# A scan layer on Trainium2: B is expanded straight from PSUM, in one go, and B and C are projected ahead of delta

## The reference, cut to what matters

```python
proj  = seq @ W_proj.T + b_proj                   # seq: (16, 1024, 192)
x_in, delta, Bm, Cm = split(proj, [192, 192, 16, 16])
delta = softplus(delta + dt_bias)
A     = -exp(A_log)                               # (192, 16)
# for every step t:
h     = exp(delta[t, :, None] * A) * h + (delta[t] * x_in[t])[:, None] * Bm[t, None, :]
y[t]  = sum over states of h * Cm[t]
out   = (y + x_in * D) @ W_out.T + b_out
```

## Time and profile before

| | us |
|---|---|
| median of 3 runs | 4584.7 (4575.44 to 4586.21) |
| profiled execution, its own time | 4598.03 |
| its span, first to last instruction | 4596.2 |
| busy: PE, DVE, ACT, POOL | 4019.0, 3294.0, 2112.8, 2494.7 |
| mean granted clock of TensorE | 0.921 |
| scans of both scan layers | from 1791.5 on, about 60% of the span |

### The profile page before, as it was taken

The page is one execution under the profiler, slowest core; times in us unless marked ns, Lnnn a source line. Parts: engine busy times, 40 slices in busy tenths (PEclk is TensorE's granted clock), DMA queues, the critical chain, the costliest instruction groups (busy, mean ns, idle before and its releaser), DMA issues. The chain is left out here.

```text
span 4596.2 us, 165194 instructions
## 1 busy us (share of the span) xinstructions
PE 4019.0 (87%) x71984; PEld 2447.8 (53%) x71984; DVE 3294.0 (72%) x3495; ACT 2112.8 (46%) x2773; POOL 2494.7 (54%) x877
## 2 busy tenths in 40 slices
PE   5994899999999966999999989995899899999998
PEld 4993666666666643444444444442454444444444
DVE  6655666767576634887877877873788778888786
ACT  2331444443434434555555555552555455555553
POOL 1111212121111203887877878883788778888886
PEclk9997999999999986899999999996799999999998
DMA  9623324233232413444434434432444444444342
GB/s 100 88 41 94 107 64 119 73 107 85 83 108 73 112 28 87 99 97 98 108 88 97 109 88 100 112 75 64 99 94 107 94 95 102 97 100 111 83 96 65
DMA packets 371280, 419.28 MB, mean 91 GB/s; under 512 B 31818, under 2 KB 284494, under 8 KB 370562
## 3 DMA queue, kind: packets, MB, share of 16 engines
q1 hardware_dynamic: 370596, 408.83, 39.2%
HBM read 267.23 MB, written 91.16 MB: 78 GB/s over the span
## 5 line engine op out<-in xcount | busy, mean ns | idle before, releaser
L1143 POOL TENSOR_TENSOR l_h<-l_h,l_c_rep 128x2048 f32<-128x2048 f32 x384 | 1768.8, 4606 | 210.3 <-DVE l_h L1062 208.3
L767 PEld LDWEIGHTS l_u_ps<-l_b_diag,l_dx_t 32*64 32x64 f32 x49152 | 836.9, 139 | 704.1 <-issue 701.3
L1062 DVE TENSOR_TENSOR_SCAN l_h<-l_decay,l_u_ps 128x512 f32<-128x512 f32 x768 | 891.3, 1201 | 376.9 <-PE l_y_ps L780 341.1
L767 PE MATMUL l_u_ps<-l_b_diag,l_dx_t 32*64 32x64 f32 x49152 | 948.5, 227 | 187.0 <-issue 105.3
L902 ACT ACTIVATE l_decay<-l_delta_rep,l_a_neg 128x1024 f32<-128x1024 f32 x768 | 858.1, 1143 | 405.3 <-DVE l_h L1062 400.4
L1062 DVE TENSOR_TENSOR_SCAN l_h<-l_decay,l_h,l_u_ps 128x512 f32<-128x512 f32 x768 | 932.0, 1254 | 9.7 <-PE l_u_ps L767 9.6
L780 PE MATMUL l_y_ps<-l_h,l_state_sum 128*64 128x512 f32 x3072 | 858.4, 685 | 11.1 <-POOL l_h L1143 11.1
L1673 ACT ACTIVATE l_probs<-l_work 128x532 f32<-128x532 f32 (+1 forms) x384 | 217.6, 567 | 559.7 <-PE l_work L1527 553.0
L780 PEld LDWEIGHTS l_y_ps<-l_h,l_state_sum 128*64 128x64 f32 x3072 | 205.0, 149 | 307.5 <-issue 264.1
L1086 DVE TENSOR_TENSOR l_b_diag<-l_b_t,l_lane 128x1024 f32<-128x1024 f32 x128 | 314.6, 2461 | 54.8 <-ACT l_b_t L954 54.8
L1842 DVE RECIPROCAL l_den<-l_den 96x1024 f32<-96x1024 f32 x32 | 209.6, 6549 | 196.3 <-ACT l_den L1686 196.3
(11 more groups left out here) (162 smaller groups left out, 5785.1 us busy)
## 6 DMA issues: line engine op xcount, KB each, us to landing
l_c_rep<-l_c_by_state SPq DMA_DIRECT2D x256, 512.0 KB, 6.5
l_delta_rep<-l_delta SPq DMA_DIRECT2D x384, 128.0 KB, 5.4
l_x<-x_after_l SPq DMA_DIRECT2D x48, 768.0 KB, 5.7
l_qk_parts<-l_qk SPq DMA_DIRECT2D x48, 768.0 KB, 4.8
l_x_res<-x_after_l SPq DMA_DIRECT2D x192, 128.0 KB
l_x<-x SPq DMA_DIRECT2D x64, 192.0 KB, 9.5
x_after_l<-l_x SPq DMA_DIRECT2D x64, 192.0 KB, 4.1
l_x_res<-x_after_l SPq DMA_DIRECT2D x16, 768.0 KB, 5.4
```

The lines of the kernel that those rows point to most:

```text
L767: made = nc.tensor.matmul(u_ps[64 * par:64 * par + 64, w % U_RING, r - 2 * win, at:at + 64], dx_t[rows, n.s, db, k, 64 * g:64 * g + 64], b ...
L1062: nc.vector.tensor_tensor_scan(h[:, s % S_RING, npi, t], decay[:, 2 * (s % 2) + npi, t], u, start, ALU.mult, ALU.add).then_inc(scanned, 1)
L1143: nc.gpsimd.tensor_tensor(view, view, c_rep[:, 2 * q:2 * q + 2, :], ALU.mult).then_inc(c_applied, 1)
```

## The change

`take_b`, ACT's copy of the transposed B out of the scratch bank into `b_t`, is gone, and with it `b_t` and the semaphore `diag_made`. DVE's `diagonals` waits for the fill itself and reads the bank. All four quarters are made one after the other behind window 11, and the last one counts the bank as drained; `fill_u` waits for that count. In the table, `bc` and `bt` move from slots 13 and 14 to 9 and 10, `de.0` from 11 to 13, and `tail.2`, the third output tile, from 9 to 14. POOL's list follows: the third residual addition goes from step 4 to 6, `finish_delta` from steps 6, 8, 9 to 7, 9, 10, `make_dx` from 7, 10 to 8, 11.

```diff
     slots = {
-        1: ["x.2"], 2: ["dx.1"], 3: ["norm"], 5: ["tail.0"], 6: ["dx.2"], 7: ["tail.1"], 9: ["tail.2"], 11: ["de.0"],
-        13: ["bc"], 14: ["bt"], 15: ["x.0"], 17: ["de.1"], 19: ["de.2"], 20: ["dx.0"], 21: ["x.1"],
+        1: ["x.2"], 2: ["dx.1"], 3: ["norm"], 5: ["tail.0"], 6: ["dx.2"], 7: ["tail.1"], 9: ["bc"], 10: ["bt"],
+        13: ["de.0"], 14: ["tail.2"], 15: ["x.0"], 17: ["de.1"], 19: ["de.2"], 20: ["dx.0"], 21: ["x.1"],
     }
...
                     if w == 0:
-                        pe.wait_ge(diag_made, n.count(1, 1))
+                        await_drained(pe, fill(n, "bt"))
...
-                def take_b(n):
-                    f = fill(n, "bt")
-                    await_fill(act, f)
-                    nc.scalar.activation(b_t[:, :], scratch[:, 0:256], ACT.Copy).then_inc(drained, 1)
-
...
                     if npq == 0:
-                        await_drained(dve, fill(n, "bt"))
-                    b = b_t[:, :].rearrange("p (c m) -> p c m", c=16)[:, :, 2 * npq:2 * npq + 2]
+                        await_fill(dve, fill(n, "bt"))
+                    b = scratch[:, 0:256].rearrange("p (c m) -> p c m", c=16)[:, :, 2 * npq:2 * npq + 2]
...
                     if npq == 3:
-                        made.then_inc(diag_made, 1)
+                        made.then_inc(drained, 1)
...
-                        if w in (16, 17, 18, 20):
-                            diagonals(after(n), (16, 17, 18, 20).index(w))
+                        if w == 11:
+                            for npq in range(4):
+                                diagonals(after(n), npq)
...
-                    if s in (2, 3, 4) and not n.first:
-                        add_residual(before(n), s - 2)
+                    if s in (2, 3, 6) and not n.first:
+                        add_residual(before(n), (2, 3, 6).index(s))
                     if not last:
-                        if s in (6, 8, 9):
-                            finish_delta(after(n), (6, 8, 9).index(s))
-                        if s in (7, 10):
-                            make_dx(after(n), s // 10)
+                        if s in (7, 9, 10):
+                            finish_delta(after(n), (7, 9, 10).index(s))
+                        if s in (8, 11):
+                            make_dx(after(n), s // 11)
```

More of the change, by code:

```diff
@@ L502, in ssm_layer @@
         b_rows = sb("b_rows", [64, HALF])
-        b_t = sb("b_t", [128, 256])
         c_rows = sb("c_rows", [128, HALF])
@@ L561, in ssm_layer @@
         dx_made = sem("dx_made")
-        diag_made = sem("diag_made")
         rows_seen = sem("rows_seen")
@@ L988, in take_slot @@
                             take_bc(of)
-                        elif kind == "bt":
-                            take_b(of)
                         elif kind == "x":
@@ L994, in take_slot @@
                             take_dx(of, int(i))
-                        else:
+                        elif kind == "tail":
                             take_output(before(n), int(i))
@@ L1004, in prologue @@
                     take_bc(n)
-                    take_b(n)
                     take_x(n, 0)
```

## The result

| | before | after |
|---|---|---|
| median, us | 4585.45 (4 runs, 4575.44 to 4588.27) | 4881.45 (4 runs, 4865.79 to 4892.88) |
| ratio | 1 | 1.0657, 95% interval 1.0626 to 1.0688 |
| profiled execution, span | 4596.2 | 4876.0 |
| mean granted clock | 0.921 | 0.882 |
| busy: PE, DVE, ACT, POOL | 4019.0, 3294.0, 2112.8, 2494.7 | 4182.4, 3148.6, 2089.7, 2396.6 |

The kernel became 6.6% slower, 296 us. The forecast of 4647 us had the sign, but the time lies far above its range, which ended at 4740. DVE and POOL lost 145 and 98 us of work, as wanted; the same matmuls kept TensorE busy for 163 us more, at a mean granted clock of 0.882 instead of 0.921.

The account below looks back on a forecast made before the run. TensorE bounds the scan layers, through its holes and clock. Per batch +3.1 - 2.6 + 2.85 - 1.5 = +1.8 us, +54 in 30 batches, +8 for prologues: 4584.7 + 62 = 4647 us, range 4555 to 4740.

Parts of the forecast that it names:

- The block's price: DVE's four diagonals in a row, read from the scratch bank: 1.11 us each, 4.44 us for the block.
- the estimate of 0.26 us more of fixed cost for the four: DVE's diagonals: by the skill's errata table, a PSUM source costs 62 cycles more, about 0.26 us for the four.
- The prologues' 8 us: Once a layer, x.0's fill waits for the diagonals: +4.2 us each less ACT's copy, +8 us in all.
- TensorE's holes for DVE at the batch's end: TensorE's waits for DVE's scans there would go: at most 2.6 us a batch, and 1.5 us of clock behind them.
- The place and the size of the stall: TensorE waits 3.1 us once a batch at window 15's u fill, for the scans of window 12 behind the block.
- SP's chain to delta 0: From POOL's last addition through SP's store, loads and C store to the end of delta 0's issues: 16.6 us.
- Hidden, with 1.2 us to spare: Batch start: first scans end 27.1 us after the third output tile; TensorE needs them after 28.3 us, so no cost.
- which nothing in my sum moves: TensorE's "issue" waits would stay at 3.6 us a batch.
- The third rival: SP's chain overruns its 1.2 us at batch starts, C loads without pause: +3 us a batch, 4737 us, chance 0.17.
- my case: Main forecast for the whole kernel: 4647 us, own range 4600 to 4707, chance 0.48.
- the clock behind the stall: Low clock behind the block's stall costs 2.85 us a batch, from eight stretches behind the loop's branch (1.65 to 4.8).
- The gain: At the batch's end, 2.6 us of waits for DVE and 1.5 us of clock go, per batch.

Follow-up runs that it names:

- the square: e5, e9, e10 and the changed kernel: third output tile in window 9 or 14, without or with the stall; ratios to before 0.990, 1.011, 1.043, 1.066.
- e5: Changed kernel with the third output tile back in slot 9 and the block of diagonals two windows later, behind window 13: 4531.84 us, ratio to before 0.990.
- e8: Changed kernel with the third output tile in slot 9, the block behind window 15, and bc, de.0, bt, x.0 in 11, 12, 13, 16: 4535.46 us.
- e2: Changed kernel with a sixteenth of the bytes in the loop batches' loads of C (the rest of C stale): 4622.94 us.
- e6: Kernel before the change with the loop batches' loads of C cut to 64 of 1024 columns (C stale): 4495.47 us.
- e9: e5 with the third output tile back in slot 14 and delta's first projection moved to 16: 4628.68 us, ratio to before 1.011.
- e10: Changed kernel with the third output tile in slot 9, B and C moved to 8, the block still behind window 11: 4770.76 us, ratio to before 1.043.
- e4: Changed kernel with only two of the four diagonals made in loop batches (the other half of the matrices stale): 4719.11 us.

## Why the prediction was wrong, point by point

**Right.** The block's price: 4.52 us from its start to that of the scans behind it, 1.13 a diagonal, against 4.44 and 1.11. (The old form is 1.14 us apart in the earlier trace rows, not 1.11, as I had read.) A diagonal's row takes 1214 ns (1210 to 1225 in all 128), the old form's in that prologue 1219 to 1225: the estimate of 0.26 us more of fixed cost for the four does not show. There are no turns with POOL, whose products are back at 4.54 us. The prologues' 8 us: TensorE waits 9.4 us there for the two blocks, where it waited 0.5 us each for ACT's copy. TensorE's holes for DVE at the batch's end are gone; the clock there is full, windows 20 to 24 lose 1.4 us of clock a batch before and none after. The place and the size of the stall: forecast 3.1 us at the third u fill behind B's transposes, found there at 3.37. And SP's chain to delta 0: the issues end 16 us after POOL's last addition, forecast 16.6, and TensorE never waits for what comes of them.

**The failed step** is "Hidden, with 1.2 us to spare", with "which nothing in my sum moves" said of the "issue" waits. I followed SP's chain only to delta 0's landing, and asked only whether the first scans come in time. The loads behind it, C's above all, were counted as free. They are eight loads of 512 KB a batch: in the kernel before they began 16 us ahead of the batch and had pauses between them; after, they follow one another around the first scan (DMA share 1.06 against 0.71), those whose landing is known take 1.5 to 2 times as long, and TensorE has holes for "issue" of up to 7 us, with low clock behind. The step was 0 in the sum, and measures 96 to 106 us. The third rival named the burst and the place, at 90 us and a chance of 0.17, and nearly hit the price. That is luck in part: its 3 us a batch were a wait for delta's landing and its clock, and TensorE never waited for that; the burst stood in it without a price of its own. Its 4737 us are my case and 90 more, so it has both causes; the 144 us from there to 4881 are the stall's clock and a gain that did not come, both below.

**The mis-sized term** is the clock behind the stall. I took the mean of the eight stretches behind the loop's branch, 2.85 us; the stretch behind the block (windows 12 to 20) loses 5.1 us a batch, above even the 4.8 of the worst of those rows (they are 15 us long, windows 12 to 20 some 28, but the low clock lies in the first 13). So the stall with its clock, forecast at 3.1 + 2.85 = 5.95 us a batch or 178 us in 30, is 3.4 + 5.1 = 8.5, or 255; the square gives 239 to 249.

**The gain** was forecast at 2.6 + 1.5 = 4.1 us a batch, less 8 for the prologues, 115 us. e5, which has it with little stall, is 1.0% or 44 us faster than before. It keeps 1.3 us of waits a batch, and its "issue" waits are 4.3 instead of 3.8: part of the gain seems to be given back at the batch's start, and more of it in e8. That fits e2 and e6, where the loads of C are small: 127 us lie between them, about what the stall (239 to 249) less the full 115 leaves. How much of the missing 71 us is which was not separated.

The sum by the measured terms: -44 for the read from the bank, 239 to 249 for the stall, 96 to 106 for the tile: 291 to 311, against 296. It is no check of its own, since the terms are the differences between before, e5, e9, e10 and after; what it shows is that the causes add.

**Open.** When C's first load begins does not alone order the kernels: e10's begins 15.2 us ahead, as early as before's 16.0, and still has 4.9 us of "issue" in windows 0 to 8 where before has 3.3. Its following loads are closer together (5.1 ahead, 2.5 ahead, 3.2 behind, against 7.9 ahead, 0.2 and 5.9 behind), which fits a quicker batch end, C; but e5's (11.8, 2.1 and 0.3 ahead, 5.4 behind) are closer still, with only 3.9 us. What else the stall does to the batch's start was not found. Nor is it known why a q8 packet comes late: whether it is asked for late or stands in a queue behind the loads.

## What to carry to other kernels

A step that is moved in a hand-written order carries its whole queue along: here one tile held back the residual, delta and C of the next batch, and the cost came as "issue" waits, which no semaphore explains and the instruction packets do. When a block of one engine's work is put in one place, look for a place where the engine that will wait has another task between the last free buffer and the one that it needs; one entry of the table moved such a task there and took back nearly all. Before you call a set of loads hidden, look at the DMA share at the place where they will land, not only at the first use.

## What the runs showed of the hardware that was not expected

- TensorE stops inside a fill, on nothing that a semaphore shows, and longer the more the loads crowd at the batch's start: 6.5 us a batch with the loads of C in one burst, 3.8 with pauses, 1.9 and 1.0 with a sixteenth of their bytes. 346 of 380 such stops end 1.20 to 1.75 us after the end of a packet of the instruction queue.
- A wait of 3.4 us costs more in clock than in itself: 5.1 us a batch behind it (after). Waits of 0.7 and 0.4 us, with a matmul group between them, cost 0.1 (e5), and waits of 0.5 to 1.2 us nothing in twelve batches (e4).
- A DVE multiply with one source in PSUM and one in SBUF, 128x1024 in float32, takes 1.214 us beside POOL. With both in SBUF it took 1.22 in a prologue without POOL beside it, and 1.190 to 3.78 in all.
